# Graph network kernel: releasing the message gathers eight products earlier

## The reference

```python
out = relu(n_feat @ lin0_w.T + lin0_b); h = out
eh = relu(e_feat @ en1_w.T + en1_b)
w_e = (eh @ en2_w.T + en2_b).reshape(-1, D, D)      # one 32x32 matrix per edge
for _ in range(STEPS):                              # 6
    msg = einsum('ei,eio->eo', out[src], w_e)
    agg = segment_sum(msg, dst, num_segments=n_nodes) + conv_bias
    m = relu(agg)
    h = _gru_cell(m, h, gru_wih, gru_whh, gru_bih, gru_bhh)
    out = h
```

## Time and profile before

| | |
|---|---|
| runs, median (lowest to highest) | 7845.22 us (7834.63 to 7847.51), 3 runs |
| the profiled execution | 7851.73 us |
| its span, first to last instruction | 7849.9 us |
| mean granted TensorE clock | 0.823 of 2.4 GHz |
| busy share | PE 70%, DVE 58%, POOL 42%, PEld and ACT 32% each |
| chain that ended last | PE 37%, DVE 17%, issue 16%, POOL 16%, DMA 9% |
| in it | DMA gathered<-table,idx_slot 3%, DMA ring<-net 2% |

### The profile page before, as it was taken

One profiled execution on the slowest core, in us unless ns is written; L12 is line 12 of the kernel. 1 busy time (PEld: TensorE's weight loads), 2 busy tenths in 40 slices (PEclk: granted clock), 3 DMA queues, 4 the chain that ended last, 5 costly groups with the idle time before them and its releaser, 6 DMA issues.

```text
span 7849.9 us, 71046 instructions
## 1 busy us (share of the span) xinstructions
PE 5507.9 (70%) x21159; PEld 2535.9 (32%) x21165; DVE 4570.4 (58%) x6775; ACT 2488.5 (32%) x4074; POOL 3321.8 (42%) x3604
## 2 busy tenths in 40 slices
PE   2996887444678555767777777766757999999940
PEld 1433443132233212222222222233545444444410
DVE  5564333133556576878888797933756466666630
ACT  1664333111233111112111212133212566666620
POOL 3777762766745442535353545454054000000036
PEclk9997887655568677989888888967978999999975
DMA  3002554233566676878778787821010000000000
GB/s 97 12 7 82 208 206 165 65 92 88 131 153 162 201 262 230 292 257 286 272 259 286 249 295 239 309 64 35 1 25 16 9 14 17 13 15 14 9 21 18
DMA packets 556450, 1015.22 MB, mean 129 GB/s; under 512 B 100911, under 2 KB 294723, under 8 KB 555556
## 3 DMA queue, kind: packets, MB, share of 16 engines
q1 hardware_dynamic: 449380, 952.53, 35.2%
q0 software_dynamic: 106688, 58.16, 4.6%
HBM read 804.42 MB, written 206.29 MB: 129 GB/s over the span
## 4 chain that ended last, share of the span: by engine, by line
PE 37%; DVE 17%; issue 16%; POOL 16%; DMA 9%; ACT 4%; SPq 1%; POOLq 0%; DVEq 0%; ACTq 0%
POOL gathered L864 9%; PE ps L999 5%; PE ps L1387 5%; DVE ring L2191 5%; PE ps L1061 4%; DMA gathered<-table,idx_slot 3%; POOL pair_slot L864 3%; DMA ring<-net 2%; PE ps L1149 2%; PE ps L1150 2%; POOL last_of L879 2%; POOL out_dram L983 2%; DVE blocks L2191 2%; PE ps L1154 2%; PE ps L1510 1%
## 5 line engine op out<-in xcount | busy, mean ns | idle before, releaser
L864 POOL DMA_INDIRECT gathered<-table,idx_slot x2156 | 2098.6, 973 | 1239.1 <-DVE ring L2191 601.1
L2191 DVE TENSOR_TENSOR ring<-ring,ps 128x1024 f32<-128x1024 f32 (+2 forms) x1008 | 1059.2, 1081 | 269.7 <-DMA ring<-net 244.4
L1061 PE MATMUL ps<-ring,mats 128*32 128x512 f32 (+2 forms) x4032 | 689.9, 640 | 333.9 <-DVE ring L2191 273.0
L999 PE MATMUL ps<-mats,gathered 128*128 128x128 f32 x1029 | 216.4, 353 | 714.8 <-DMA gathered<-table,idx_slot 673.1
L978 POOL COPY idx_slot<-idx_run_end 128x16 int32<-128x16 int32 (+2 forms) x14 | 2.7, 195 | 1556.0 <-SPq L846 1538.2
L857 POOL COPY idx_slot<-idx_row 128x16 int32<-128x16 int32 (+2 forms) x154 | 31.1, 202 | 1041.9 <-SPq L578 1003.1
L999 PE MATMUL ps<-mats,w 128*128 128x128 f32 x736 | 178.2, 394 | 392.7 <-DVE w L2694 249.6
L2258 DVE SCALAR_TENSOR_TENSOR x_block<-ps,bias,blocks 128x512 f32<-128x512 f32 x300 | 224.7, 749 | 381.4 <-PE ps L1154 381.2
L999 PEld LDWEIGHTS ps<-mats,gathered 128*128 128x128 f32 x1029 | 143.5, 175 | 875.4 <-DMA gathered<-table,idx_slot 772.1
L1061 PEld LDWEIGHTS ps<-ring,mats 128*32 128x32 f32 x4032 | 154.0, 123 | 809.1 <-issue 516.3
L1387 PE MATMUL ps<-w,en 128*128 128x512 f32 (+2 forms) x896 | 381.2, 586 | 0.0
(11 more groups left out here) (303 smaller groups left out, 11958.2 us busy)
## 6 DMA issues: line engine op xcount, KB each, us to landing
ring<-net SPq DMA_DIRECT2D x792, 512.0 KB
blocks<-net SPq DMA_DIRECT2D x264, 512.0 KB
net<-ring SPq DMA_DIRECT2D x176, 512.0 KB, 2.9
gathered<-table,idx_slot POOLq DMA_INDIRECT x2352
ring<-net SPq DMA_DIRECT2D x144, 256.0 KB
table<-w SPq DMA_DIRECT2D x143, 256.0 KB, 2.7
ring<-d_sp SPq DMA_DIRECT2D x100, 256.0 KB, 4.3
x_sp<-x_block SPq DMA_DIRECT2D x79, 256.0 KB, 4.2
```

Source lines behind the costliest of these rows:

```text
L864: pool.indirect_dma_start(dests(k), None, rows, bass.IndirectOffsetOnAxis(ap=dst[:, k:k + 1], axis=0)).then_inc(done, 16)
L999: last = nc.tensor.transpose(dst[:, k * P:k * P + P], src[:, k * P:k * P + P], mat["ident"])
L1061: last = mm(message[t * D:t * D + D, 0:wd(i)], adders[2 * m + c], ring[slot][:, c * wd(i):(c + 1) * wd(i)], start=(m == 0 and c == 0), sto ...
L2191: v.tensor_tensor(pair, pair, state, ALU.mult).then_inc(sig["pr"][S_], 1)
```

## The change

A transfer of a gather waits for the product that stands eight places in front of the one that it waited for. Where k is 8 or more that is product k minus 8 of the same block i minus 2, else product 8 + k of block i minus 3. The first eight transfers of block 2 wait for no product. The wait of the index copy for the buffer, the order of the transfers and all other engines' programs are as they were; the passes outside P5 to P10 have no `pace` and are not touched.

```diff
@@ -82,6 +82,7 @@
 WIDE = 8
 CHUNKS = D * D // P
 PAIRS = T * CHUNKS // 2
+LEAD = PAIRS // 2
@@ -858,8 +859,9 @@
                 pool.wait_ge(s_slot, i * per + (base + sub + 1))
                 settle(pool)
                 for k in range(tl(i)):
-                    if pace and i > 1:
-                        pool.wait_ge(sig["pr"][S_], pace.n("pr", S_, i - 2, k) + 1 + CREDIT)
+                    if pace and i > 1 and (i, k) >= (2, LEAD):
+                        front = (i - 2, k - LEAD) if k >= LEAD else (i - 3, PAIRS + k - LEAD)
+                        pool.wait_ge(sig["pr"][S_], pace.n("pr", S_, *front) + 1 + CREDIT)
                         settle(pool)
                     pool.indirect_dma_start(dests(k), None, rows, bass.IndirectOffsetOnAxis(ap=dst[:, k:k + 1], axis=0)
                                             ).then_inc(done, 16)
```

## The result

| | before | after |
|---|---|---|
| runs, median (lowest to highest) | 7839.93 us (7831.51 to 7847.51), 4 runs | 7777.73 us (7766.19 to 7786.57), 4 runs |
| the profiled execution | 7851.73 us | 7786.57 us |
| its span | 7849.9 us | 7784.8 us |
| mean granted TensorE clock | 0.823 | 0.829 |

What follows compares the result with a forecast made beforehand. It took late gathers, whose heads hold up DVE in the six message passes, as the removable loss, with DVE the bound in good seams. 26 + 22 + 10 = 58 us off 7845.2 gave 7787 us, range 7757 to 7823.

Steps and rivals of the forecast that it cites:

- The mechanism: Message passes: the head waits for its gather's last transfer; released half a block earlier, 13.7 us, it lands in time.
- Issue to head: Seam of P5: from the issue of the gather's last transfer to the head's start, read from the trace as 5.5 us.
- P5, 26 us predicted: P5, blocks 2 to 11: late heads' waits go, 25 us by DVE and 28 by PE, taken as 26.
- 1.5 us stay: P5 seams: `conv_sum` wait left after the change, 0.81 + 0.67 us for a full head, ten times 15.
- P6 to P10, blocks 3 to 11, 22 us predicted: 45 blocks of 1259.2 us fall to the undisturbed 27.48 us each, 1236.8; bounds 0 and 85 us.
- Starts, 10 us predicted: Starts of passes: only gather 3 gains, its last transfer 2.5 us earlier; between 0 and 12.5 us for five passes.
- About 50 us left: Sign of being right: of the heads' 228.5 us of waits for gathers, about 50 us stay in all.
- a new wait of the same size in front of [...] edge sum 0: Sign of being wrong: the removed wait turns up again in front of product 8 or edge sum 0.
- Only P5 gains: Rival: in P6 to P10 the DVE bound or seam copies take back the gain; 26 us, 7819; chance 0.14.
- More than the wait: Rival: the undisturbed block itself gets shorter, so all PE waits count; 123 us, 7722; chance 0.13.
- Slower by the clock: Rival: PE idles before edge sum 0 in P6 to P10, which runs at 1.2 GHz; 7890 us; chance 0.04.
- It does nothing: Rival: something ending at the same time as the gather held the head; 7845 us; chance 0.08.

Runs made afterwards that it cites:

- p5_only: Changed kernel with the lead of eight products in P5 alone, P6 to P10 waiting as before: 7817.62 us, 0.9958 of the kernel before.
- last_late: Changed kernel, but the last transfer of each gather waits for product 15 of block i minus 2 as before: 7819.75 us, 0.9963 of the kernel before.
- gru_only: Changed kernel with the lead of eight products in P6 to P10 alone, P5 waiting as before: 7817.61 us, 0.9957 of the kernel before.
- later: Waits of the kernel before, but each gather's last transfer waits one product longer, for product 0 of block i minus 1: 7959.49 us, ratio 1.0141.
- lead16: Changed kernel with a lead of 16 products, a whole block, instead of eight: 7777.06 us, 0.9907 of the kernel before.
- unpaced: Changed kernel with no waits for products, only the free buffer holding a gather back: 7779.10 us, 0.991 of the kernel before.
- second_half: Changed kernel, but only transfers 8 to 15 of a gather lead by eight products, 0 to 7 wait as before: 7785.44 us, ratio 0.9919.
- sum_first: Kernel before, with edge sum 0 put ahead of the next block's head and reset gate in P6 to P10: 7931.43 us, ratio 1.0096.

## Why the prediction was right

- **The mechanism.** That a head waits for the last transfer of its gather, and that an earlier release takes this wait away, is shown for P5 by `p5_only` and `last_late`. For P6 to P10 `gru_only` shows that the earlier release is what helps and `later` that a late head reaches product 8, but `last_late` that the place of the other transfers, which the prediction didn't price, has a part in it. Issue to head was read as 5.5 us; the lone transfer of `last_late` took 5.75 under much the same traffic. By the rule of the Trainium skill (DMA: Bandwidth & Descriptors, Anatomy of one DMA), 2.0 us plus the bytes, the transfer of the earlier trace rows would have been in time and the change would have given nothing; it gave 62.2 us, so here the trace was the right guide. That moving the stream of transfers does no new harm held in `lead16` and `unpaced`.
- **P5, 26 us predicted.** Blocks 2 to 11 went from 377.6 us (38.19 + 339.37) to 344.9 (32.56 + 312.31), 32.7 less, over the upper bound of 28. The term that was mis-sized is "1.5 us stay": `conv_sum` waits 4.9 us in all ten seams together, not 15. The 0.67 us added for a full head are the difference of 1.11 and 0.44; but 1.11 is the length of a head at the lower clock level, behind a wait. The ten heads, of four transposes each, took 9.7 us in all (five of them 1.11 or more) and take 6.6, each 0.65 or 0.66. So the bound by PE's own 28.2 us of waiting left out 3.1 us of slow heads; the two make 31.3 of the 32.7. By DVE's waits, 40.0 - 4.9 = 35 us, the working comes out somewhat over the measured.
- **P6 to P10, blocks 3 to 11, 22 us predicted.** 18.2 measured, 25.5 in `gru_only`, 26.9 in `second_half`, with a spread of some 6 us between executions: 22 was a good middle. P8 gave 13.8 us of it, of which 5.6 had gone in `p5_only` without the change; P9 gave 4.3 of the 7.4 expected. DVE's bound holds the rest at 27.2 to 27.8 us a block.
- **Starts, 10 us predicted.** From the first product of a pass to block 3, the five passes took 376.4 us before and 371.9 after, 4.6 less. The 2.5 us a pass were sized by POOL's issues alone, and that the whole of it reaches the time had no row. The heads did come that much earlier: they wait 105.2 us there instead of 115.3, head 3 alone 25.1 instead of 34.0. Less than half of it came through. In P6 the last transfer of gather 3 is issued at 3130.77, 15 times 1.25 us after the first as worked out, and head 3 still waits 4.57 us: the head of block 3 is held by POOL's rate, and heads 1 and 2 as they were.
- **The sum.** 58 against 62.2 us by the medians and 65.1 by the profiles. The three terms measured 32.7 + 18.2 + 4.6 = 55.5 us instead of 26 + 22 + 10; the other 9.6 lie where the prediction had no term: blocks 12 and 13 of all six passes (6.1), the first two blocks of P5 (1.2), and the stretches between and outside the passes. P5 was too low by 7, the rest of the terms too high by 9, and that the total came so near is in part luck.
- **"About 50 us left" of the heads' waits** was wrong, 111.7 are left. It did not follow from my own numbers, which had 115 us at the starts of P6 to P10; those stayed for the most part (20.9 us at the start of P6 against the 23.0 of the earlier trace rows). The sign of being wrong, "a new wait of the same size in front of [...] edge sum 0", did appear in part: PE's idle time in front of edge sum 0 in the 45 blocks went from 9.4 to 63.6 us. It cost nothing, so that was no sign of the time getting longer.
- **The rivals.** Only P5 gains: fell with `gru_only` (0.9957). More than the wait: fell, since P6 to P10 gave 27.4 us in all and the 77.3 us of head waits in their full blocks were nearly three times that. Slower by the clock: the idle time did move in front of edge sum 0, but only 1.4 us a block (from 0.2), and none of the 45 edge sums ran at the lower level; the granted clock of these stretches is 0.93 to 0.95 and was 0.91 to 0.94. The mechanism is real: in `sum_first`, with 4.0 us in front of it, edge sum 0 ran at the lower level in all 45. It does nothing: fell with the result.

## What to carry to other kernels

A gather is as late as its last transfer, and the last transfer can be late by the product that it waits for and by what stands in front of it on the engine that issues it. When a paced stream feeds something that comes right at the end of the pace, count from the last transfer's issue, as the trace has it, to the use, and give it a lead of that length. Here two products were enough, more bought nothing, and a last transfer one product later cost 109 us; what lies between 0 and 2 was not run. The same late us has different prices: on a path that DVE reads at once every us counts, on one with slack behind it only a part does, so price them by stretch and not by the sum of the waits. And a matmul group whose length was read behind a wait may be a slow one: take the length of an undelayed group for what will stay.

## What was not expected of the hardware

- Removing a wait in front of a short group of matmuls made the group itself shorter. The ten heads of P5, 40 transposes, as min, median and max in ns, before (first line) and after:

```profile
L999 PE MATMUL ps<-mats,gathered x40: 272/421/477, 2666.4 to 3005.8; 128*128 128x128 f32 x40
```

```profile
L1001 PE MATMUL ps<-mats,gathered x40: 272/273/330, 2661.1 to 2972.2; 128*128 128x128 f32 x40
```

  The granted clock over the late head of the earlier trace rows (3005.08 to 3006.19) is 0.50, the 1.2 GHz level, and over the head at 2903.57 of the kernel after 1.00, the 2.4 GHz level; that of the nine blocks went from 0.72 to 0.78. In `later` all 40 ran at 421 ns or more. But the length of the wait alone does not decide it: in the seam of `last_late` shown above a head took 0.65 us at a granted clock of 1.00 after 3.40 us of idle time, and the one of the kernel before 1.11 after 3.29.
- An indirect DMA of 16 KB issued with nothing in front of it on POOL took 5.75 us to the matmul that reads it, while 512 KB ring tiles were being loaded, with 269 GB/s moved in that stretch. The indirect transfers into `pair_slot` of the kernel before, which run from 389 to 667 us with the DMA engines busy for 0.07 of the time, land 2.4 us after their issue by the median. They differ in what they move, so that the traffic makes the difference is likely and not shown.
- 16 such transfers in one burst beside those loads did not delay the loads in a way that shows: 207.7 us of ring waits in `unpaced`, 205.0 with the pacing.
